# Lag search spectra in other PSUM banks, key and value splitting on GpSimd, two layer norms folded into scales, fp16 lag-weight transforms, and a new order of the work on every engine

## The reference

```python
x = x + autocorrelation(norm(x), ctx, ctx)      # a: top 9 lags of each channel's circular correlation
x = x + base_and_lora(norm(x))                  # b: x @ W_base.T + b_base, plus top-2 of 8 rank-16 experts
x = x + windowed_attention(norm(x), ctx)        # b/c: 8 heads over 128 channels, window of 16 of 1024 places
x = x + lora_only(norm(x))                      # c: top-2 of 4 rank-16 experts
```

## Time and profile before

| | |
|---|---|
| median of 3 runs | 1870.63 us |
| profiled execution / its span | 1869.2 us / 1867.4 us |
| PE busy | 1708.1 us (91%), 19296 matmuls |
| PE weight loads | 1082.9 us (58%) |
| DVE busy | 1569.8 us (84%), 4726 instructions |
| ACT busy | 1165.5 us (62%) |
| POOL busy | 905.9 us (49%), 870 instructions |
| mean granted PE clock | 0.971 |
| chain that ended last | PE 56%, DVE 19%, ACT 9%, POOL 8%, issue 6% |
| DMA | 549359 packets, 111.37 MB, 531088 packets under 512 B |

### The profile page before, as it was taken

How to read it: one execution, slowest core, us unless ns; L and a number is a source line. 1 busy time by engine, 2 the same in 40 slices (tenths; PEclk the granted TensorE clock), 3 DMA queues, 4 the chain that set the end, 5 groups by cost and what they waited for, 6 DMA issues and landing times.

```text
span 1867.4 us, 48204 instructions
## 1 busy us (share of the span) xinstructions
PE 1708.1 (91%) x19296; PEld 1082.9 (58%) x19296; DVE 1569.8 (84%) x4726; ACT 1165.5 (62%) x1929; POOL 905.9 (49%) x870
## 2 busy tenths in 40 slices
PE   3689999999999999999999999999999999999975
PEld 2356566666556666556666655666665566665553
DVE  6778898888889888888888888988888888888853
ACT  5257666666666665765666676666666566667642
POOL 2445544455554545555455555444555545455432
PEclk8799999999999999999999999999999999999985
DMA  5133322333332233332223333223334322333220
GB/s 208 34 58 69 58 50 48 54 69 69 69 48 47 54 61 69 69 58 53 48 51 69 69 69 57 49 48 55 69 69 64 51 48 48 67 69 58 29 30 24
DMA packets 549359, 111.37 MB, mean 60 GB/s; under 512 B 531088, under 2 KB 531344, under 8 KB 548624
## 3 DMA queue, kind: packets, MB, share of 16 engines
q1 hardware_dynamic: 549136, 108.29, 30.7%
HBM read 57.94 MB, written 16.78 MB: 40 GB/s over the span
## 4 chain that ended last, share of the span: by engine, by line
PE 56%; DVE 19%; ACT 9%; POOL 8%; issue 6%; DMA 1%; SPq 0%; DVEq 0%; ACTq 0%; POOLq 0%
PE pb L601 18%; PE pc L674 8%; ACT q_diag L876 6%; POOL rest L1422 4%; PE pa L561 4%; POOL prob L1422 4%; PE pa L523 3%; PE pa L497 3%; PE pa L524 3%; PE pa L498 3%; PE pa L499 3%; ACT v_im L778 3%; PE pb L590 2%; DVE rows_c L1249 2%; DVE x_c L1141 2%
## 5 line engine op out<-in xcount | busy, mean ns | idle before, releaser
L601 PE MATMUL pb<-w_base_h,even_words 128*128 128x512 f16 x1024 | 324.8, 379 | 0.0
L1459 POOL TENSOR_TENSOR sc<-sc,sc_rec 128x512 f32<-128x512 f32 x128 | 134.1, 1048 | 294.6 <-DVE sc_rec L1236 294.6
L876 ACT ACTIVATE q_diag<-sc,par 32x512 f32<-32x512 f32 x384 | 268.8, 715 | 10.3 <-DVE sc L1149 3.1
L1429 POOL TENSOR_TENSOR p_hl<-sc,p_hl 128x512 f16<-128x512 f32 x128 | 164.3, 1283 | 208.0 <-ACT p_hl L778 208.0
L601 PE MATMUL pb<-w_base_l,even_words 128*128 128x512 f16 x512 | 193.9, 379 | 0.0
L488 PE MATMUL pa<-xn_a,tab 128*128 128x512 f32 x384 | 181.7, 610 | 4.6 <-ACT xn_a L778 4.6
L674 PEld LDWEIGHTS pc<-sc_t,v_diag 128*128 128x128 f16 x6144 | 170.1, 97 | 20.6 <-DVE sc_t L1243 6.0
L674 PE MATMUL pc<-sc_t,v_diag 128*128 128x32 f16 x6144 | 173.9, 177 | 5.6 <-DVE sc_t L1243 5.6
L652 PE MATMUL pc<-k_h,q_diag 128*128 128x32 f16 x2048 | 169.2, 177 | 0.0
L653 PE MATMUL pc<-k_l,q_diag 128*128 128x32 f16 x2048 | 168.5, 177 | 0.0
L654 PE MATMUL pc<-k_h,q_diag 128*128 128x32 f16 x2048 | 168.5, 177 | 0.0
(11 more groups left out here) (166 smaller groups left out, 4619.6 us busy)
## 6 DMA issues: line engine op xcount, KB each, us to landing
x_a<-in_x SPq DMA_DIRECT2D x32, 512.0 KB, 5.5
x_res<-in_ctx_in SPq DMA_DIRECT2D x32, 512.0 KB, 5.1
x_res<-in_x SPq DMA_DIRECT2D x32, 512.0 KB, 3.7
v_diag<-even_words SPq DMA_DIRECT2D x128, 128.0 KB, 4.9
v_diag<-p_hl SPq DMA_DIRECT2D x128, 128.0 KB, 4.9
out<-rows_c SPq DMA_DIRECT2D x32, 512.0 KB, 2.6
v_diag<-in_base_w SPq DMA_DIRECT2D x4, 1024.0 KB, 10.0
q_diag<-in_ra SPq DMA_DIRECT2D x1, 544.0 KB, 13.7
```

Of the source, the lines that this page charges most:

```text
L601: mm(pb[:, h, :], rows[:, cols], weights[:, j, h * HALF:(h + 1) * HALF], start=(j == 0 and m == 0), stop=False)
L876: nc.scalar.activation(q_diag[rows, blocks, col:col + QB], source, ACT.Copy, scale=par[rows, a:a + 1]).then_inc(qd_out.sem, 1)
L1429: g_.tensor_tensor(part[:, :, :, LO], sc[:, g % 2, :, :], part[:, :, :, HI], ALU.subtract)\
```

## The change

1. **Banks.** The context's spectrum goes to `pa[2:4]` and waits for the four lag products (`prod_w`); the query's spectrum goes to `pa[0:2]` and waits for the residual (`x1_out`). The long spectrum of the context now waits for the three copies `v_out` instead of the products. `a_context` stands ahead of `a_aggregate`, and ACT's `a_values` is moved to the start of its next step.
2. **Keys and values.** ACT evicts each in fp32 to `kv_f` (the tile of `xn_b`); POOL makes both fp16 parts. DVE's two instructions go. The value eviction waits for `kl_out`, that is for POOL's second key instruction.
3. **Queries.** POOL's four pieces of `q_diag` go. SP places them with two DMAs (`place_queries`), which need no parity mask. On SP the order is now: x_res, even values, x of the next sample, queries, context of the next sample, odd values, output.
4. **Norms 1 and 3.** The column mean of the weights is taken off the weights once (`weight_means` on PE, `centre_weights` on DVE, inside the first steps), the transposes take the raw rows, and the reciprocal root is multiplied in later: in the first operation of `gates` and in the scale of `b_base` and `c_result`. `b_norm_rows` of norm 1 and `c_norm_rows` go. `root` makes one more 128x1 value for norms 1 and 3. `gates` of the last layer now waits for `ln_rs3`.
5. **Lag weights.** Transposed weights are split in fp16 (ACT the high part, DVE `a_transposed_low` the low one), and the two tables are stored in two fp16 parts: three fp16 products in place of one fp32.
6. **Order.** All lists are rewritten. `b_router` moves to the end of PE's step. POOL starts a step with the two `a_sum`, then `root` of norm 3.

The core of the diff (the last function is POOL's; its `b_keys` is the same with `k_h` and `k_l`):

```diff
             def a_context(b, slot):
...
-                    pe.wait_ge(x1_out.sem, x1_out.after(b - 1))
-                project_ctx(0, slot, CTX_FWD).then_inc(mm_ctx.sem, 1)
+                    pe.wait_ge(prod_w.sem, prod_w.after(b - 1))
+                project_ctx(2, slot, CTX_FWD).then_inc(mm_ctx.sem, 1)
...
             def a_weights(b, n):
-                if n == 0:
-                    pe.wait_ge(wt_out.sem, wt_out.after(b))
-                    project(pa, 2, wt, tab[:, WEIGHTS_IM, :]).then_inc(mm_wim.sem, 1)
...
+                for h in range(2):
+                    cols = slice(h * HALF, (h + 1) * HALF)
+                    mm(pa[:, place + h, :], w_ctx_h[:, table, :], wt_h[:, cols], start=True, stop=False)
+                    mm(pa[:, place + h, :], w_ctx_l[:, table, :], wt_h[:, cols], start=False, stop=False)
+                pe.wait_ge(wtl_out.sem, wtl_out.after(b))
+                for h in range(2):
+                    cols = slice(h * HALF, (h + 1) * HALF)
+                    last = mm(pa[:, place + h, :], w_ctx_h[:, table, :], wt_l[:, cols], start=False, stop=True)
...
+            def weight_means():
+                pe.wait_ge(ones_set.sem, 1)
+                pe.wait_ge(w_in.sem, 16 * (SPLITS + 4))
...
+                for h in range(2):
+                    for j in range(KT):
+                        at = j * D + h * HALF
+                        last = mm(pc[:, h, :], ones_mean, base_f32[:, at:at + HALF],
+                                  start=(j == 0), stop=(j == KT - 1))
+                last.then_inc(w_mean.sem, 1)
...
+            def place_queries(b):
+                sp.wait_ge(ql_out.sem, ql_out.after(b))
+                sp.wait_ge(qdiag_set.sem, 1)
+                if not first(b):
+                    sp.wait_ge(mm_sc.sem, mm_sc.after(b - 1))
+                for head in (2 * MOVED_PAIR, 2 * MOVED_PAIR + 1):
+                    rows = slice(HD * head, HD * (head + 1))
+                    sp.dma_start(q_diag[rows, :, rows], q_hl[rows, :].rearrange("p (n t) -> p n t", t=QB))\
+                        .then_inc(q_placed.sem, 16)
...
                 if live(2):
-                    place_values(i - 2, 1)
+                    place_queries(i - 2)
                 if live(-1):
                     load_ctx(i + 1)
+                if live(2):
+                    place_values(i - 2, 1)
...
+            def a_transposed_low(b):
+                for h in range(2):
+                    cols = slice(h * HALF, (h + 1) * HALF)
+                    dve.wait_ge(wth_out.sem, wth_out.after(b, h + 1))
+                    v.tensor_tensor(wt_l[:, cols], pa[:, 2 + h, :], wt_h[:, cols], ALU.subtract)\
+                        .then_inc(wtl_out.sem, 1)
...
+            def centre_weights():
+                dve.wait_ge(const_in.sem, CONSTS_IN)
+                dve.wait_ge(w_mean.sem, 1)
...
+                for rows, column_mean in centred:
+                    v.tensor_tensor(rows, rows, column_mean.unsqueeze(1).to_broadcast(list(rows.shape)),
+                                    ALU.subtract).then_inc(w_centred.sem, 1)
...
             def gates(b, n, source, experts):
...
+                if n == 0:
+                    dve.wait_ge(ln_scale[1].sem, ln_scale[1].after(b))
+                else:
+                    dve.wait_ge(ln_rs[3].sem, ln_rs[3].after(b))
...
             def b_values(b):
                 act.wait_ge(mm_v.sem, mm_v.after(b))
+                act.wait_ge(kl_out.sem, kl_out.after(b))
+                nc.scalar.activation(kv_f[:, :], pa_hi, ACT.Identity, bias=bias_att[:, 2:3]).then_inc(vf_out.sem, 1)
...
+            def b_values(b):
+                pool.wait_ge(vf_out.sem, vf_out.after(b))
+                if not first(b):
+                    pool.wait_ge(vt_out.sem, vt_out.after(b - 1))
+                g_.tensor_copy(v_halves[:, PAD:PAD + D, HI], kv_f[:, :]).then_inc(vh_out.sem, 1)
+                pool.wait_ge(vh_out.sem, vh_out.after(b))
+                g_.tensor_tensor(v_halves[:, PAD:PAD + D, LO], kv_f[:, :], v_halves[:, PAD:PAD + D, HI],
+                                 ALU.subtract).then_inc(vl_out.sem, 1)
```

More of the change, by code:

```diff
@@ L234, in build @@
         rs_y = [little(1) for n in range(4)]
+        rs_w = [little(1) for n in range(4)]
+        unscaled = little(1)
         rs_less = little(1)
@@ L287, in build @@
         ln_rs = [signal(f"ln_rs{n}") for n in range(4)]
+        ln_scale = [signal(f"ln_scale{n}") for n in range(4)]
         ln_less = signal("ln_less")
@@ L704, in step @@
                 if live(2):
-                    b_router(i - 2)
+                    b_keys(i - 2, odd)
+                if live(3):
+                    c_scores(i - 3, 3)
+                if live(2):
+                    b_base(i - 2, 1, 0)
+                    b_values(i - 2, odd)
                 if live(3):
@@ L973, in step @@
                     a_transposed(i - 1, 1)
+                if first(i - 1):
+                    split_weights()
                 if live(2):
@@ L985, in step @@
                 if live(3):
-                    experts_exp(i - 3, 1, pc, E1)
+                    spread(i - 3, 3, rows_c, squares_c, 1 - odd)
                 if live(2):
@@ L1281, in step @@
                     c_subtract(i - 2, 2)
+                    c_transpose(i - 2, 0)
+                    c_sums(i - 2, 2)
+                if live(0):
+                    a_top(i, 0)
                 if live(1):
                     gates(i - 1, 0, pb, E0)
+                if live(-1):
+                    variance(i + 1, 0)
                 if live(2):
-                    c_sums(i - 2, 2)
                     c_scores(i - 2, 3)
+                if live(0):
+                    a_top(i, 1)
+                if live(2):
+                    c_subtract(i - 2, 3)
+                    c_transpose(i - 2, 1)
+                    c_sums(i - 2, 3)
                 if live(0):
@@ L1298, in step @@
                     a_ninth(i)
+                    a_softmax(i)
+                if first(i - 0):
+                    centre_weights()
                 if live(2):
                     c_transpose(i - 2, 3)
+                if live(1):
+                    b_base(i - 1, 1 - odd)
+                    mean(i - 1, 2, x2_out)
+                    b_values(i - 1, 0)
                 if live(0):
-                    a_softmax(i)
+                    a_transposed_low(i)
+                if live(2):
+                    c_attention_residual(i - 2, odd)
+                if live(1):
+                    b_norm_rows(i - 1, 1 - odd)
+                if live(0):
+                    a_products(i, 0)
+                    a_products(i, 1)
+                    a_products(i, 2)
+                if live(2):
+                    mean(i - 2, 3, x3_out)
+                if live(0):
+                    a_products(i, 3)
+                if live(1):
+                    b_queries(i - 1)
                 if first(i - 0):
@@ L1488, in step @@
                     c_low(i - 1, 0)
+                if first(i - 0):
+                    clear_queries()
+                if live(1):
                     c_normalise(i - 1, 1)
+                if live(0):
+                    root(i, 1)
+                if live(1):
+                    c_normalise(i - 1, 2)
+                if live(0):
+                    b_keys(i)
+                if live(1):
                     c_low(i - 1, 1)
-                    c_normalise(i - 1, 2)
                     c_low(i - 1, 2)
+                if live(0):
+                    b_bias(i)
+                if live(1):
                     c_normalise(i - 1, 3)
+                if live(0):
+                    b_values(i)
+                if live(1):
                     c_low(i - 1, 3)
```

345 lines of the change are left out of this document (149 added, 196 removed).

## The result

The changed kernel took 1917.46 us (median of 4 runs, 1913.32 to 1919.09) against 1869.9 for the kernel before: a ratio of 1.0253 [1.0232, 1.0273]. It is slower by 2.5%, where the prediction had it 0.6% faster. The profiled execution took 1919.09 us, its span is 1917.3 us.

A forecast was written before the change was run, and what follows sets the result against it. A loop of waits through several engines and SP's DMAs, six parts summing to 54.5 us a step, was taken as the bound: 1869.2 - 14 over 29 steps + 1 for the ends = 1856 profiled, 1858 median; range 1812 to 1893.

The forecast's parts named there:

- Part 2: SP's queue: after the residual, context load issue 1.5 us, then four value DMAs landing in 8.5 to 9; 10.0 us.
- part 1: From the end of B's last lag product on DVE to the residual, with gates waiting for norm 3's root; 7.8 us.
- part 3: From the values' landing through b_features on ACT to the first subtraction of the next step; 5.3 us.
- part 4: From that first subtraction over DVE and ACT work to the evicted values; 12.8 us.
- part 5: From evicted values through POOL's copy and low part, then c_low colliding with the softmax, to softmax end; 6.9 us.
- part 6: From the softmax's end over POOL's normalise, context and roots and DVE's products to the loop's start; 11.7 us.
- The copies are dear: Rival: POOL's value copy takes 2.14 us, adding 1.25 a step, 1894 us; decided from about 1.3; chance 0.28.
- Values in time: Rival: value DMAs land before ACT asks, part 2 is covered, step 53.35 us, time 1825; chance 0.16.
- Softmax not blocked: Rival: DVE's softmax meets POOL idle, 1.3 us less in part 5, time 1820; chance 0.13.
- PE's floor of 51.3: PE's own work per step: 52.2 us busy less 0.85 saved on the lag weights.
- The ends: Start 8 us longer (0 to 17) for column means and centring, end 7 shorter; together about +1 us.
- The drain's -7: End of the run: c_norm's stage goes, and PE's wait for it; 7 us off, between 3 and 10.

The follow-up runs named there:

- e2: Changed kernel with the exponentials left in place in PSUM, so the softmax has one operand in SBUF; 1892.87 us.
- e1: Changed kernel with SP's order put back: odd values issued before the next context's load; 1845.09 us.
- e9: Changed kernel with the last values' four DMAs ahead of the context's load on SP, but behind the same wait for the residual; 1845.05 us.
- e7: Changed kernel with GpSimd's strided copy of the values made twice; 1970.53 us.
- e6: Changed kernel with values before context loads on SP, exponentials in PSUM, ACT's constants wait a step later, GpSimd's last root between the two aggregation additions; 1813.9 us.

## Why the prediction was wrong, step by step

**The loop was the right one, and one term of it was mis-sized.** Part 2, "10.0 us on SP", took 11.0 in the step shown and, as a mean, 0.33 + 11.2 = 11.5, with the handoffs 11.6. Its two terms were 1.5 for the load's issue, which measured 0.33, and 8.5 for the four value DMAs, which measured 11.2. I had said that "four value DMAs take 5.6 to issue, the last about 1.5 of that, and land 4.9 later, so 8.5 to 9". These are the times of the four with the context's load behind them. The change puts 512 KB right in front of them, and I priced that load by its issue alone. With 11.6 in its place the sum is 54.5 + 1.6 = 56.1; 56.27 was measured. The text even said that "the landing of DMAs is a queue that I know only as a median", but drew from it only a rival on the fast side and a spread up to 1874 us.

The other parts, forecast and as measured in the steps shown: part 1 7.8 and 7.8 (DVE idle 1.9 where 1.4 was said); part 3 5.3 and 5.5; part 4 12.8 and 13.0; part 5 6.9 and 6.8; part 6 11.7 and 11.5.

**Part 5 had the right length by another path**, and that was luck. I let the softmax follow GpSimd's copy and low part. It follows ACT's two times four exponentials instead. The copies took 1.33 us (values, to every second place) and 1.04 (keys), not 0.9, and neither is in the chain of the step shown. The collision with `c_low`, 1.3 in the forecast, was there and cost 1.2. By the Trainium skill (SBUF — State Buffer, "SBUF: two separate sides") such a pair excludes each other for the whole length; e2 bears that out, since one operand in PSUM ends it. The estimates from the Trainium skill's other page (GPSIMD Engine Reference, "Performance versus the Vector engine"), 0.9 and 2.2 us, enclose the two copies, and neither is right.

**The rivals.** *The copies are dear* forecast the right side (1894) for the wrong reason: it was to decide from 1.3 us of copy, and the copy took 1.33, but the copy isn't in the chain, and e1 and e9 win the loss back with the copy as it is. How much of its 0.4 us too many comes back through the softmax, as in e7, no run shows. Its chance was 0.28, and the range's upper end of 1893 lay just under its 1894. *Values in time* is e1 and e9: 53.8 us a step, where I had worked out 53.35. It is the state that the kernel would have been in without the load in front. *Softmax not blocked* is e2, worth 0.75 a step and not 1.3. PE's floor of 51.3 was not reached by any run: e6's step is 53.03, with PE idle for 1.7.

**The ends.** The centring was put at 8 us between 0 and 17; it costs 11.1. ACT's wait was not costed at all: `a_values` of sample 0 moved to the beginning of ACT's step 1, and with that behind the wait for the constants, 13.3 us. The forecast's +8 became +20.4. The drain's -7 was right in size (-6.8). In the last step PE's wait ahead of the last transposes fell from 4.66 us to 1.39; where the rest comes from was not followed.

With both corrections, 1858 + 29 x 1.6 + 12.4 = 1917. The range's lower part went to faster loops; part 2's bound for the four DMAs, "8.5 to 9", reached 0.5 us above its central value where 2.7 was needed, though this was the one part whose surroundings the change altered.

## What to carry to other kernels

The duration of a DMA, read from a trace, holds for what stood in front of it in its queue there; when the order of issues changes, price what is in front (here some 1.25 us for each 256 KB of load), not the issue of the load. A transfer that somebody waits for goes ahead of a bulk load that nobody does yet, even if both are free to start at the same moment. And an engine's waits for constants belong on the list of moved steps: look at what is now behind them.

## What was not expected of the hardware

A 512 KB load whose own issue takes 0.33 us and that is issued right ahead of them lengthened the four 128 KB DMAs behind it from 8.7 to 11.2 us, and 256 KB from 8.7 to 9.9. When the load stands behind them (e9) its own issue takes 1.0 to 2.9 us, and the step is none the longer for it. A GpSimd copy of 1024 columns from fp32 to fp16 takes 1.04 us into neighbouring places and 1.33 into every second one. An extra instruction of 1.33 us that nobody waits for lengthened the step by 1.75: 1.2 through what it pushed into a collision, and a part of the rest went with the half clock that PE was granted after it had idled.
